# The mixer's slots with output tiles: another order of VectorE's and ScalarE's work

## The reference

```python
h = x * rsqrt(mean(x * x) + EPS) * norm_w
proj = einsum('bsd,od->bso', h, in_proj_w)           # gate, hBC, dt
hBC = silu(causal_conv(hBC, conv_w, conv_b))         # 4 taps along the sequence
hid, B, C = split(hBC)
dt = softplus(dt + dt_bias); A_cs = cumsum(-exp(A_log) * dt)
# per head: y[i] = sum over j <= i of (C[i] . B[j]) * exp(A_cs[i] - A_cs[j]) * dt[j] * hid[j]
y = y + Dp * hid
yg = y * silu(gate)
yg = yg * rsqrt(mean over the group of yg * yg + EPS) * gnorm_w
out = einsum('bsd,od->bso', yg, out_proj_w)
```

## Time and profile before

| | us |
|---|---|
| median of 3 runs (2739.1 to 2741.68) | 2739.22 |
| the profiled execution: time | 2737.24 |
| its span | 2735.3 |
| PE busy | 2318.3 (85%) |
| DVE busy | 1987.0 (73%) |
| ACT busy | 1466.0 (54%) |
| POOL busy | 1226.2 (45%) |

### The profile page before, as it was taken

How to read it: one execution, slowest core, us unless ns; L and a number is a source line. 1 busy time by engine, 2 the same in 40 slices (tenths; PEclk the granted TensorE clock), 3 DMA queues, 4 the chain that set the end, 5 groups by cost and what they waited for, 6 DMA issues and landing times. The chain is left out here.

```text
span 2735.3 us, 33995 instructions
## 1 busy us (share of the span) xinstructions
PE 2318.3 (85%) x11172; PEld 1670.5 (61%) x11172; DVE 1987.0 (73%) x3158; ACT 1466.0 (54%) x3097; POOL 1226.2 (45%) x772
## 2 busy tenths in 40 slices
PE   5956667766532999999999999999999999889997
PEld 4532222225422777777777777777777777568996
DVE  4569989983534787586686785776776866788777
ACT  2344434443102696595685785876865956742221
POOL 2229988981000364364362462552634633542112
PEclk9989999998665999999999999999999999889999
DMA  2040030001032242232231231322322312220110
GB/s 79 25 124 0 0 123 0 0 3 59 28 129 71 86 129 73 61 113 65 73 113 54 85 96 55 103 71 80 105 66 69 109 61 74 74 79 24 47 47 32
DMA packets 117378, 183.59 MB, mean 67 GB/s; under 512 B 9760, under 2 KB 77728, under 8 KB 116192
## 3 DMA queue, kind: packets, MB, share of 16 engines
q1 hardware_dynamic: 117216, 181.55, 20.8%
HBM read 170.90 MB, written 10.62 MB: 66 GB/s over the span
## 5 line engine op out<-in xcount | busy, mean ns | idle before, releaser
L78 PE MATMUL mg_pb<-xT2h,mg_wh 128*128 128x512 f32 x1152 | 479.6, 416 | 17.2 <-POOL mg_wl L1265 17.2
L1275 POOL TENSOR_TENSOR mg_y<-mg_hT,mg_sg 128x512 f32<-128x512 f32 x128 | 187.6, 1466 | 626.2 <-DVE mg_hT L1511 576.4
L79 PE MATMUL mg_pb<-xT2l,mg_wh 128*128 128x512 f32 x1152 | 454.0, 394 | 0.0
L80 PE MATMUL mg_pb<-xT2h,mg_wl 128*128 128x512 f32 x1152 | 452.0, 392 | 0.0
L784 PE MATMUL ss_y<-ss_pr,cst 128*128 128x512 f32 x512 | 278.2, 677 | 125.9 <-POOL ss_pr L766 125.8
L1486 DVE TENSOR_TENSOR mg_m<-mg_gb,mg_cb 128x384 f32<-128x384 f32 x512 | 267.6, 550 | 150.8 <-ACT mg_gb L1662 74.4
L1459 DVE SCALAR_TENSOR_TENSOR mg_hT<-mg_pb,mg_cw,mg_hT 128x510 f32<-128x510 f32 (+2 forms) x432 | 320.7, 743 | 33.5 <-ACT mg_hT L1612 23.3
L766 POOL TENSOR_TENSOR ss_pr<-o,ss_bc 128x1024 f32<-128x1024 f32 x128 | 301.4, 2370 | 46.3 <-DVE o L735 26.8
L784 PEld LDWEIGHTS ss_y<-ss_pr,cst 128*128 128x128 f32 x512 | 98.5, 210 | 305.4 <-POOL ss_pr L766 225.6
L666 ACT ACTIVATE ss_da<-dt,ss_na 128x510 f32 (+1 forms) x256 | 165.9, 680 | 207.9 <-DVE o L735 207.9
L78 PEld LDWEIGHTS mg_pb<-xT2h,mg_wh 128*128 128x128 f32 x1152 | 217.3, 189 | 76.6 <-issue 19.2
(11 more groups left out here) (291 smaller groups left out, 5199.2 us busy)
## 6 DMA issues: line engine op xcount, KB each, us to landing
mg_abc<-acs_rows SPq DMA_DIRECT2D x256, 256.0 KB, 3.4
mg_ws<-in_w_in SPq DMA_DIRECT2D x72, 512.0 KB, 3.6
ss_bc<-bc_rows SPq DMA_DIRECT2D x16, 1024.0 KB, 6.4
mg_wos<-in_w_out SPq DMA_DIRECT2D x64, 256.0 KB, 3.7
ff_ws<-in_w SPq DMA_DIRECT2D x7, 1024.0 KB, 4.8
x<-in_x SPq DMA_DIRECT2D x16, 256.0 KB, 4.1
ip_ws<-in_w_in SPq DMA_DIRECT2D x8, 512.0 KB, 3.6
x_kept<-x SPq DMA_DIRECT2D x2, 2048.0 KB, 7.2
```

Source lines behind the costliest of these rows:

```text
L78: pe.matmul(out, lhs[0], rhs[0], start=start, stop=False)
L79: pe.matmul(out, lhs[0], rhs[1], start=False, stop=False)
L80: return pe.matmul(out, lhs[1], rhs[0], start=False, stop=stop)
L1275: pool.tensor_tensor(yb[:, p % RING, t], hT[s % 2][:, t], sg[s % 2][:, t], ALU.mult).then_inc(s_y2, 1)
```

## The change

In the slots that have a pair and output tiles VectorE and ScalarE get an order of their own; in all other slots the instructions and their order are as before. No instruction is added or taken out, and TensorE, GpSimd and SyncE are the same. VectorE's second scaling `times_step(p,1)` and the remainder `low` of the first tile go ahead of the clamp of batch 1 and of batch 1's kernels 2 and 3, the three taps of a tile are taken apart, and `skip(p,0)` goes ahead of kernels 6 and 7. ScalarE makes `high` of the first tile and the first tap ahead of exponentials 2 and 3, and `high` of the second tile ahead of exponentials 6 and 7.

```diff
@@ VectorE's loop over the slots
                     bc = is_bc(s)
+                    if outs and p is not None:
+                        times_step(p, 0)
+                        kernel_of(p, 0)
+                        kernel_of(p, 1)
+                        times_step(p, 1)
+                        low(*outs[0])
+                        clamp(p, 1)
+                        tap(1, s, 0)
+                        kernel_of(p, 2)
+                        kernel_of(p, 3)
+                        tap(2, s, 0)
+                        tap(3, s, 0)
+                        tap(1, s, 1)
+                        kernel_of(p, 4)
+                        kernel_of(p, 5)
+                        clamp(p, 3)
+                        tap(2, s, 1)
+                        tap(3, s, 1)
+                        add(*outs[0])
+                        low(*outs[1])
+                        skip(p, 0)
+                        kernel_of(p, 6)
+                        kernel_of(p, 7)
+                        add(*outs[1])
+                        skip(p, 1)
+                        continue
                     if p is not None:
                         clamp(p, 1)
                         times_step(p, 0)
...
                         times_step(p, 1)
-                        if outs:
-                            low(*outs[0])
                         taps(s, 0)
...
                         kernel_of(p, 7)
-                        if outs:
-                            add(*outs[0])
-                            low(*outs[1])
                         skip(p, 0)
...
-                        if outs:
-                            add(*outs[1])
                         skip(p, 1)
@@ ScalarE's loop over the slots
                         decay(p, 0)
                         decay(p, 1)
+                        if outs:
+                            high(*outs[0])
+                            first_tap(s, 0)
+                            decay(p, 2)
+                            decay(p, 3)
+                            first_tap(s, 1)
+                            decay(p, 4)
+                            decay(p, 5)
+                            high(*outs[1])
+                            decay(p, 6)
+                            decay(p, 7)
+                            silu(s, 0)
+                            silu(s, 1)
+                            gate(s, 0)
+                            gate(s, 1)
+                            continue
...
                         decay(p, 3)
-                        if outs:
-                            high(*outs[0])
                         first_tap(s, 0)
...
                         decay(p, 7)
-                        if outs:
-                            high(*outs[1])
```

## The result

The changed kernel takes 2711.34 us as the median of 4 runs (2709.99 to 2715.22), the kernel before in the same comparison 2739.16: a ratio of 0.9899, 95% interval 0.9882 to 0.9916. It is faster by 27.8 us, 1.0% (by the interval, 23 to 32 us). The medians alone could not tell a gain of 24.8 us from one of 27.8; the lengths of the slots in the traces can. The profiled execution took 2712.28 us with a span of 2710.4. In one later run, the kernel before with GpSimd held back, one execution of four took 12316 us and is left out of its figures.

What follows compares the result with a forecast made beforehand. The prediction took TensorE's pace to bound the mixer, with only its queue's pauses to win: 13.4 + 6.8 + 2.9 + 1.7 = 24.8 us, so 2739.22 - 24.8 = 2714.4 us, range 2711.5 to 2722.5.

Steps and rivals of the forecast that it cites:

- Pause ahead of turn(p,1): Second and third slots: transposes wait for times_step(p,0) behind clamps stretched by GpSimd; 0.96 us lost in each of 14.
- The lock between VectorE and GpSimd: Shared port pair held for a whole instruction; read from two long clamps (1.35, 1.06 us) and a 3.31 us remainder.
- Its warning for low(0) in a third slot: low(0) now falls near GpSimd's chain; worst case 3.31 us long, losing 4 x 0.3 = 1.2 us.
- First slots, 7 x 0.97 = 6.8 us: Seven first slots: out_tile 0 waits for low(0), as high(0) stands behind exponentials 2 and 3; 0.97 us each.
- the tight slack of 0.4 us: First slots: low(0) ends at 6.9 us, TensorE reaches out_tile 0 at 7.3; with two-piece remainders the slack is 0.2.
- the rival that they keep their stall: First slots: high(0) or low(0) over 0.4 us later than walked, giving back up to 7 us: 2721.5 us; chance 0.12.
- The 0.42 us per two-piece group: Four groups with two-piece remainders take 0.42 us longer per three slots; expected to go with the pauses, 1.7 us.
- The walk through the slot: Start and end times forecast for each moved instruction in a touched slot, from its first transpose as t = 0.
- out_tile 1: lost 0.14 us, 21 x 0.14 = 2.9 us: All 21 touched slots: out_tile 1 starts 0.37 us after the last projection, where 0.23 would do, waiting for low(1).
- The forecast of 26.8 to 26.9 us per slot: Expected length of each touched slot after the change; three of them 80.5 us in place of 83.84.
- Slower: Rival: tile 0's taps end after 16.7 us, projection 3 stalls in all 21 slots; 2750 us, chance 0.06.

## Where the prediction was right, and the step that failed

- That TensorE bounds the mixer and that only pauses of its queue can be won: right. It is busy 80.16 of 80.16 us now, and the gain is all in the 21 slots.
- Pause ahead of turn(p,1), 14 x 0.96 = 13.4 us: right in cause, and in the size of the gap. The clamp back in front gives 1.0 us per slot back, holding GpSimd alone takes the same 1.0 us away.
- The lock between VectorE and GpSimd: it was read from four rows and the experiment with GpSimd held confirms it. The Trainium skill ("SBUF — State Buffer", section "Who interferes with whom") says that the second of the two to issue blocks until the first is done. The traces agree, down to a clamp instruction of 2.40 us beside a GpSimd instruction of 2.42. Its warning for low(0) in a third slot was worth 0.1 us: it took 1.32 us (from 1139.21) instead of 1.21, and ended 5.8 us into the slot, where I had taken 5.9.
- First slots, 7 x 0.97 = 6.8 us: right in size, with the tight slack of 0.4 us holding; the rival that they keep their stall did not come true. The run with only these slots old shows 1.2 to 1.4 us each, this pause and that of the second output tile together. The cause was read by half: VectorE, with kernels 2 and 3 and the second scaling, came free 0.11 us behind the end of high(0), so the orders of both engines held low(0).
- The 0.42 us per two-piece group, 4 x 0.42 = 1.7 us: right; all seven groups now take 80.16 to 80.17 us.
- The walk through the slot: times_step at 0.8, low(0) at 4.4, the clamp at 5.6, low(1) at 14.4, skip(p,0) at 16.9 us were forecast; the trace has 0.8, 4.5, 5.6, 14.4 and 16.8.
- The step that failed is the price of a pause in the sum, above all in the term "out_tile 1: lost 0.14 us, 21 x 0.14 = 2.9 us". I took the gap alone and left out what follows it. The run with the late remainder measured 0.25 us for it, so 21 x 0.25 = 5.2 us in place of 2.9. The kernel before shows the missing part: its output tile 1 starts at 1126.74, and its second matmul 0.34 us later, as in the run with the late remainder, against 0.24 in the changed kernel. That is 0.10 us in each of 21 slots. Behind each of the 14 pauses ahead of the transposes the next transpose came 0.03 us later too (0.14 us after the first, now 0.11): 2.1 + 0.4 = 2.5 us. In the first slot of g = 6 the second output tile had waited 0.3 us longer than in the others. With these the sum is 24.8 + 2.5 + 0.3 = 27.6 us, against 27.7 in the traces and 27.8 in the medians. The forecast of 26.8 to 26.9 us per slot was off for the same reason (26.70 and 26.73).
- The range: its lower end allowed 2.9 us of gain beyond the sum, for shorter pauses elsewhere and not for the slow step behind a pause, which alone was worth 2.5. It was also too tight for the scatter of the medians: of the changed kernel's two, 2711.34 lies 0.2 us outside and 2712.53 inside. That the time fell so near the edge is chance; that the sum was about 3 us short is not, since the slots show it.
- "Slower", batch 1's chain holding up tile 0's taps: not in these slots, by the slack of 6 to 7 us that the walk gave (tile 0's taps end 9.5 us into the second slot, forecast 9.6); it did come true in the slots with r = 0, where that cover is missing and GpSimd stretches the moved clamp.

## What to carry to other kernels

Where one engine is the bound, walk its queue from start to start and give each pause a producer; then look at how long the producer's neighbours took against their usual time, since a stretched instruction points to another engine. If it does, try to hold that engine's work back first: one wait on the engine with slack did half of what the reordering did, and in two slots of group 0, without an output tile to hide moved work, it brought 6.7 to 8.3 us where moving the clamp brought 2.7 to 4.2 (the spread is that of the third slot's clock). When pricing a pause, compare the steps behind it with those of a slot without the pause, and add what is slower; here that was 0.10 us at one place and nothing at another.

## What the runs showed of the hardware

- A wait on TensorE can cost more than its gap. Ahead of out_tile 1 it made the second matmul of the waiting group come 0.34 us after the first instead of 0.24, and the slots with and without the wait differ by the sum (0.25 for a gap of 0.14). In the trace the weights of the first matmul were loaded 0.22 us ahead of it without the wait, and with it only at its start. At out_tile 0 the second matmul came 0.33 to 0.34 us after the first in all slots, so a wait there cost its gap alone.
- Four 128x128 clamps of 0.28 us took 0.8 us without GpSimd beside them, 2.6 with two of its instructions, 4.5 to 4.6 with longer ones.
- Behind a step of 3.08 us ahead of the transposes in group 0 (TensorE idle for 2.69 of them) matmuls of 0.23 us spacing came every 0.43. The granted clock was 1.00 over the 2.8 us of the pause, 0.50 (the lower of its two levels, 1.2 GHz) from 941.30 to 944.10 and 1.00 again from 944.50 on; over the slot it was 0.91, and 1.00 when the pause was gone.
- The third slot of that group took 18.1 us in some executions and 19.6 in others, of kernels that are alike there. The clock makes the difference: over this slot it was 1.00 in the kernel before (18.11 us, behind a step of 2.74 us) and 0.91 in the changed one (19.63 us, behind a step of 2.69), with 0.50 from 961.60 to 964.60. What decides whether it falls behind such a pause stays open.
